# Mixtures of eight in tiles of 128 rows, second-layer weights held in SBUF, the first opening on four batches

## The reference, cut to what matters

```python
scores = xf @ Wr + br                                # 4096 tokens, 8 experts
_, top_idx = jax.lax.top_k(scores, 2)
router_weights = softmax(where(mask(top_idx), scores, -inf))
h = gelu(einsum('td,edp->etp', xf, W1) + b1[:, None, :])     # 128 -> 512, tanh form
y = einsum('etp,epd->etd', h, W2) + b2[:, None, :]           # 512 -> 128
out = einsum('te,etd->td', router_weights, y)                # x + 0.5 * out
```

## Time and profile before

| | |
|---|---|
| time, three runs | 1420.34, 1422.12, 1422.55 us; median 1422.12 |
| profiled execution | span 1422.4 us; the page gives no time around it |
| busy, share of the span | PE 83%, PEld 55%, DVE 58%, ACT 51%, POOL 51% |
| chain that ended last | PE 54%, DVE 14%, POOL 10%, DMA 8%, issue 6%, ACT 5%, SP's queue 3% |
| first mixture of eight on TensorE | about 77 to 242 us |
| second mixture of eight on TensorE | about 718 to 893 us |

### The profile page before, as it was taken

The page is one execution under the profiler, slowest core; times in us unless marked ns, Lnnn a source line. Parts: engine busy times, 40 slices in busy tenths (PEclk is TensorE's granted clock), DMA queues, the critical chain, the costliest instruction groups (busy, mean ns, idle before and its releaser), DMA issues.

```text
span 1422.4 us, 23037 instructions
## 1 busy us (share of the span) xinstructions
PE 1176.4 (83%) x7234; PEld 782.2 (55%) x7234; DVE 825.7 (58%) x2697; ACT 721.3 (51%) x1451; POOL 721.7 (51%) x949
## 2 busy tenths in 40 slices
PE   4289997899999999999789998329999777389994
PEld 3278986122233232232278987218799556268894
DVE  7611265898898999998442666702216687421235
ACT  4244443477767767677544555213445575234441
POOL 3776754202424435523764477744554277625543
PEclk9999999699999999999979999659999898589997
DMA  9577887535435343341357886425577031145586
GB/s 292 149 198 213 243 234 243 163 102 167 133 103 174 103 118 118 88 136 49 117 140 222 258 234 185 146 78 167 161 211 245 28 132 36 49 133 177 175 260 199
DMA packets 166377, 226.82 MB, mean 159 GB/s; under 512 B 22960, under 2 KB 125744, under 8 KB 166256
## 3 DMA queue, kind: packets, MB, share of 16 engines
q1 hardware_dynamic: 121456, 174.04, 42.3%
q0 software_dynamic: 18304, 37.65, 7.7%
q10 hardware_dynamic: 26496, 13.64, 3.3%
HBM read 152.81 MB, written 72.20 MB: 158 GB/s over the span
## 4 chain that ended last, share of the span: by engine, by line
PE 54%; DVE 14%; POOL 10%; DMA 8%; issue 6%; ACT 5%; SPq 3%; ACTq 0%; POOLq 0%; DVEq 0%
PE PS L1416 17%; PE PS L1406 16%; POOL dispatched L736 8%; DVE arena L2300 5%; PE PS L1584 5%; PE PS L1560 5%; DMA arena<-experts 3%; ACT arena L1131 2%; PE PS L1396 2%; PE PS L1568 2%; PE PS L1546 2%; DMA YC<-expert_out 1%; DVE BST L1858 1%; DVE X L1868 1%; DMA expert_out<-arena 1%
## 5 line engine op out<-in xcount | busy, mean ns | idle before, releaser
L1004 ACT ACTIVATE arena<-PS,arena 128x256 f32<-128x256 f32 (+1 forms) x568 | 267.4, 498 | 367.7 <-PE PS L1406 355.8
L764 POOL DMA_INDIRECT expert_out<-arena x316 | 304.5, 964 | 281.7 <-issue 192.9
L1131 ACT ACTIVATE arena<-PS 128x512 f32<-128x512 f32 x512 | 283.9, 596 | 134.8 <-PE PS L1560 133.9
L2300 DVE TENSOR_REDUCE arena<-PS 128x2 f32<-128x1024 f32 x256 | 300.9, 1217 | 28.8 <-PE PS L1570 27.9
L1406 PE MATMUL PS<-arena 128*128 128x256 f32 (+1 forms) x1136 | 309.0, 415 | 9.8 <-DMA arena<-experts 7.5
L1416 PEld LDWEIGHTS PS<-arena 128*128 128x128 f32 x2528 | 303.9, 192 | 18.7 <-issue 4.0
L1416 PE MATMUL PS<-arena 128*128 128x128 f32 x2528 | 306.7, 275 | 3.2 <-DVE arena L2123 3.2
L2123 DVE TENSOR_TENSOR arena<-PS,arena 128x256 f32<-128x256 f32 (+1 forms) x142 | 64.5, 454 | 369.5 <-PE PS L1416 369.5
L1406 PEld LDWEIGHTS PS<-arena 128*128 128x128 f32 x1136 | 210.0, 195 | 59.8 <-DMA arena<-experts 10.1
L736 POOL DMA_INDIRECT dispatched<-arena x192 | 185.3, 965 | 81.7 <-issue 57.9
L1560 PE MATMUL PS<-arena 96*128 96x512 bf16 x512 | 174.2, 391 | 10.5 <-ACT arena L1131 4.7
(11 more groups left out here) (274 smaller groups left out, 1177.3 us busy)
## 6 DMA issues: line engine op xcount, KB each, us to landing
arena<-experts SPq DMA_DIRECT2D x142, 578.0 KB
qk_products<-arena SPq DMA_DIRECT2D x48, 384.0 KB, 4.4
arena<-qk_products SPq DMA_DIRECT2D x64, 288.0 KB
arena<-dispatched SPq DMA_DIRECT2D x110, 129.0 KB, 3.0
dispatched<-FILL SPq DMA_DIRECT2D x32, 322.5 KB, 2.8
YC<-expert_out ACTq DMA_DIRECT2D x40, 256.0 KB
arena<-qk_products SPq DMA_DIRECT2D x64, 128.0 KB, 5.1
arena<-dispatched SPq DMA_DIRECT2D x32, 193.5 KB, 4.0
```

Of the source, the lines that this page charges most:

```text
L764: pool.indirect_dma_start(YK, bass.IndirectOffsetOnAxis(ap=ID[:, s:s + 1], axis=0), YS[:, s, :], None).then_inc(s_yo[r], 16)
L1004: act.activation(HT[:, tau % PAIR, q, 0:S * P], hidden_chunk(S, q), func, bias=WE[:, r, 2 * DFF + q:2 * DFF + q + 1]).then_inc(s_g, 1)
L1131: act.activation(PT[:, G % 2, j, k, :], bank(4 + k % 2), ACT.Exp, scale=float(1.0 / np.sqrt(HD))).then_inc(s_exp, 1)
L2300: dve.tensor_reduce(MX[:, G % 2, head:4:2, a], PS[:, 1024 * w:1024 * w + 1024].rearrange("p (a b) -> p a b", a=2), AX_X, ALU.max).then_inc ...
```

## The change

Tiles of the mixtures of eight have 128 rows (`S0 = 1`), so there are 71. Each expert's second-layer weights (262 KB) are loaded once for each mixture to a fixed place in SBUF: for the first mixture at the start, before anything is cleared, for the second in the last groups of the attention. The table holds the place of these weights instead of the expert's number; TensorE loads it into a register for each tile and addresses the moving operand of the second layer by it. SP takes the expert from the row number (regions now have 8192 rows) and issues three DMAs for a tile: rows, biases (behind the rows in the same ring) and first-layer weights. Weights are asked for when the hidden layer of the tile four before is done. The 16 clears move from the opening into the loop of the first mixture, the stores of the first attention batch behind the loop, the loads of expert outputs in mid-mixture from ACT to SP, the filling of the stacks from POOL to DVE. The first mixture opens on four batches and 25 tiles, the second on 12 tiles; all steps laid between tiles are spread over twice the number, POOL sends one block for a tile. At the end of the attention the table of all tiles is computed in three parts between tiles. Two tiles share a scatter semaphore.

The diff, cut to its core:

```diff
-E0, S0 = 8, 2
+E0, S0 = 8, 1
...
-REGION = TOKENS + S0 * P
+REGION = 2 * TOKENS
...
-KNOWN = 5
-SOON = 12
+KNOWN = 4
+SOON = 25
 LEAD = 4
-BEGUN = 6
+BEGUN = 12
...
+SPLIT_AT, RING_AT, BEHIND_AT = 35062, 12310, 26754
+PLACES = [[RING_AT + RING * UP + DOWN * n for n in range(5)] + [BEHIND_AT + DOWN * n for n in range(3)],
+          [SPLIT_AT + DOWN * n for n in range(E0)]]
...
             if b >= NG - 2:
-                return MOE[0]["tiles"] + 1 + 2 * (b - NG + 2)
+                return MOE[0]["tiles"] + 1 + 4 * (b - NG + 2)
             if carries(L):
-                return max(tiles_to(b) + 4, early_tiles(L) + E0 + 3 + 2 * b)
-            return max(tiles_to(b) + 6, early_tiles(L) + E0 + 4 + 2 * b)
+                return max(tiles_to(b) + 8 + b, early_tiles(L) + E0 + 6 + 4 * b)
+            return max(tiles_to(b) + 12, early_tiles(L) + E0 + 10 + 4 * b)
...
         @block.sync
+            def expert_stays(f, e):
+                at = PLACES[first_kind(f)][e]
+                sp.dma_start(arena[:, at:at + DOWN], ex0_in[e, :, UP:UP + DOWN]).then_inc(s_stay, 16)
+
+            for e in range(E0):
+                expert_stays(0, e)
             sp.wait_ge(s_zero, 1)
             sp.wait_ge(s_fill0, 1)
-            for e in range(E1):
-                clear_experts(BUFS[1], e, s_cleared)
...
+            def eight(L):
+                def rows_in(tau):
+                    if tau < tiles:
+                        r = tau % XRING
+                        t, n = (TS0, tau) if tau < soon else (TS, tau - soon)
+                        row = sp.value_load(t[n:n + 1, 0:1], min_val=0, max_val=E0 * REGION - S0 * P)
+                        found[tau] = row // REGION
+                        sp.dma_start(XP[:, r, 0, :], BUFS[0][bass.ds(row, P), :]).then_inc(s_rows[r], 16)
+                        sp.dma_start(biases(f, tau), ex0_in[bass.ds(found[tau], 1), :, UP + DOWN:WROW]
+                                     .rearrange("o p n -> p (o n)")).then_inc(s_rows[r], 16)
+
+                def ups_in(tau):
+                    sp.dma_start(ups(f, tau), ex0_in[bass.ds(found[tau], 1), :, 0:UP].rearrange("o p n -> p (o n)"))                      .then_inc(s_we[tau % RING], 16)
+
+                def follow(tau, rows=True):
+                    sp.wait_ge(s_h, (T0 + tau - (RING - 1)) * FC)
+                    ups_in(tau)
+                    if rows:
+                        sp.wait_ge(s_yc, T0 + tau - RING)
+                        rows_in(tau + XRING - RING - 1)
...
+                lead = XRING - RING - 1
+                for tau in range(RING):
+                    rows_in(tau)
+                    ups_in(tau)
+                for tau in range(RING, RING + lead):
+                    rows_in(tau)
+                clear_tails()
+                for tau in range(RING, soon - lead):
+                    follow(tau)
...
+                for tau in range(soon - lead, tiles):
+                    follow(tau)
+                    if f == 0 and 0 <= tau - soon < E1:
+                        clear_experts(BUFS[1], tau - soon, s_cleared)
+                    for b in range(combined_within(L)):
+                        if start_of(L, b) == tau:
+                            wait_outputs(sp, f, outputs_of(L, b))
+                            load_outputs(sp, L, b)
+                if prepares(L):
+                    first_stacks()
+                    sp.wait_ge(s_fill, 2 * QK_RING)
+                    sp.wait_ge(s_qd, STORES)
+                    load_stacks(0)
+                for b in (NG - 2, NG - 1):
+                    wait_outputs(sp, f, outputs_of(L, b))
+                    load_outputs(sp, L, b)
...
         @block.gpsimd
-                    for n in range(2 if tau < tiles - 4 else 0):
-                        if carries(L) and place_of(L, sent // (2 * GT)) <= tau:
-                            send_next(sent)
-                            sent += 1
+                    if carries(L) and tau < tiles - 8 and place_of(L, sent // (2 * GT)) <= tau:
+                        send_next(sent)
+                        sent += 1
...
         @block.tensor
+            def find_expert(f, tau, soon):
+                stays[f, tau] = pe.value_load(stay_of(tau, soon), min_val=0, max_val=ARENA - DOWN)
+
+            def downs(f, tau, q):
+                if moe_of(f)["E"] == E0:
+                    return arena[:, bass.ds(stays[f, tau] + q * D, D)]
+                return WE[:, tau % RING, UP + q * D:UP + q * D + D]
...
                         mm = pe.matmul(bank(6, P * s, P * s + P), HT[:, tau % PAIR, q, P * s:P * s + P],
-                                       WE[:, r, DFF + q * D:DFF + q * D + D], start=(q == 0), stop=(q == FC - 1))
+                                       downs(f, tau, q), start=(q == 0), stop=(q == FC - 1))
...
                     if c <= tiles:
                         outputs(c - 1)
+                        find(c + 1)
...
         @block.vector
-                rows_turned(f, 1)
-                main_table(f, bank(5, 0, NG * E0), True)
+                main_counts(f, bank(5, 0, NG * E0), True)
                 rows_turned(f, 2)
                 outputs_out(f, 0)
+                main_sums()
+                rows_turned(f, 3)
+                outputs_out(f, 1)
+                main_rows(f)
+                rows_turned(f, 4)
+                outputs_out(f, 2)
                 even_gates(f)
```

More of the change, by code:

```diff
@@ L110, in constants @@
     put("spare", PAIRS + np.arange(BLOCKS)[None, :] * P + p[:, None])
-    put("segrow", np.append(np.tile(np.arange(E0) * REGION, NG), E0 * REGION))
-    put("segstep", np.tile(np.where(np.arange(E0) < E0 - 1, 1, 1 - E0), NG) * (np.arange(NG * E0) < NG * E0 - 1))
+    put("segrow", np.append(np.tile(np.arange(E0) * REGION, NG), SPARE_AT))
+    for n, places in enumerate(PLACES):
+        steps = np.tile(np.roll(places, -1) - np.array(places), NG)
+        put(f"segplace{n}", steps * (np.arange(NG * E0) < NG * E0 - 1))
     put("tile", p[:, None])
@@ L239, in build @@
         behind = cv.at
+        assert behind == BEHIND_AT
         cv = Carver()
@@ L373, in row_loads, with each, stay_of, biases @@
         def row_loads(f, tau):
-            before = sum(len(range(tau % XRING, moe_of(j)["tiles"], XRING)) for j in range(f))
-            return (tau % XRING < XCHUNKS) + before + tau // XRING + 1
+            def each(j):
+                return 2 if moe_of(j)["E"] == E0 else 1
+            before = sum(each(j) * len(range(tau % XRING, moe_of(j)["tiles"], XRING)) for j in range(f))
+            return (tau % XRING < XCHUNKS) + before + each(f) * (tau // XRING + 1)
+        def stay_of(tau, soon):
+            t, n = (ET0, tau) if tau < soon else (ET, tau - soon)
+            return t[n:n + 1, 0:1]
+        def biases(f, tau):
+            if moe_of(f)["E"] == E1:
+                return WE[:, tau % RING, UP + DOWN:WROW]
+            return XP[:, tau % XRING, 1:3, :].rearrange("p a b -> p (a b)")[:, 0:NARROW]
+        def ups(f, tau):
+            if moe_of(f)["E"] == E1:
+                return WE[:, tau % RING, 0:UP]
+            return arena[:, RING_AT + UP * (tau % RING):RING_AT + UP * (tau % RING + 1)]
         def scattered0(f, r):
@@ L381, in scattered, with shared_by, sign_of @@
         def scattered(f, r, n):
-            return sum(16 * size(f, tau) for tau in range(r, n, out_ring(f)))
+            return sum(16 * size(f, tau) for tau in range(n) if sign_of(f, tau) == r)
+        def shared_by(f):
+            return PAIR if moe_of(f)["E"] == E0 else 1
+        def sign_of(f, tau):
+            return tau % out_ring(f) // shared_by(f)
         def out_ring(f):
@@ L636, in moe @@
[L636 to L645, removed]
@@ L659, in moe @@
-                if f == 0:
-                    sp.wait_ge(s_cleared, CLEARED)
-                for tau in range(soon, XRING if not soon else ahead + XRING - RING):
+                for tau in range(RING):
+                    expert_in(tau)
+                sp.wait_ge(s_disp, sent_for(L))
+                for tau in range(XRING):
                     rows_in(tau)
-                for tau in range(max(ahead, RING), tiles):
+                for tau in range(RING, tiles):
                     sp.wait_ge(s_yc, T0 + tau - (RING - 1))
@@ L711, in attention @@
                         store(b + 1)
+                    if 0 <= G - (GROUPS - 6) < 4:
+                        sp.wait_ge(s_qd, STORES * NG)
+                        for e in range(2 * (G - (GROUPS - 6)), 2 * (G - (GROUPS - 6)) + 2):
+                            expert_stays(ffn_of(L + 1), e)
             for L, kind in enumerate(SUBLAYERS):
-                if kind in (FFN0, FFN1):
-                    moe(L)
+                if kind == FFN0:
+                    eight(L)
+                elif kind == FFN1:
+                    sixteen(L)
                 elif kind == ATTN:
@@ L1499, in open_keys_values, with find @@
                     mm.then_inc(s_lk, 1)
+                def find(tau):
```

(5 more changed lines are left out.)

267 lines of the change are left out of this document (127 added, 140 removed).

## The result

The changed kernel takes 1466.78 us (median of four runs, 1463.23 to 1469.38), the kernel before 1421.59 beside it: ratio 1.0295, interval 1.026 to 1.033. The forecast had the sign and the engine, but 18 us where 45 came.

What follows compares the result with a forecast made beforehand. TensorE bounds the mixtures at 3.73 us per tile; after the change SP was to pace them at 2.32. First mixture +14.6 us and second +3.2 sum to 17.8, so 1440 us, range 1402 to 1468.

Steps and rivals of the forecast that it cites:

- SP paces: Both mixtures: SP's register load and three issues take 2.32 us per tile, over TensorE's 1.89; chance above break-even 0.67.
- no waits of SP in either mixture: Sign that the forecast is right: SP issues without waiting in both mixtures, three issues each 2.3 us.
- the first rival: Both mixtures: issues overlap or cost under 1.89 us per tile, so TensorE sets the pace; 1399 us, chance 0.18.
- Break-even at 2.2: Rival for SP's pace in both mixtures: at 2.2 us per tile nothing is won or lost, 1422 us; chance 0.08.
- 6 loads of outputs: First mixture, SP's queue: six loads of expert outputs formerly issued by ScalarE, estimated at 1.3 us each, 7.8 in all.
- the 16 clears moved from the opening into the loop: First mixture, SP's queue: each clear costs an issue and a gap of 0.44 us, 7 us in all.
- All these fit into 2.32 us per tile: Items put at nothing, among them ScalarE's and VectorE's work per tile, stay hidden; at 1.89 they would begin to show.
- The stores: End of first mixture: six stores of the first attention batch behind the loop, 3.4 us of issues and a landing of 6.
- The second mixture: Last weights leave SP at 893.7, last bias add 900.2, then POOL's 38 sends until 948.3: +3.2 us.
- The opening: First mixture opens on four batches, 32 sends instead of 40, so SP's wait ends at 60.8 instead of 70.92.
- TensorE paces: Faster rival, both mixtures: issues cost under 1.89 us per tile, each mixture 11.4 us shorter; 1399 us, chance 0.18.
- Exposed register loads: Rival, both mixtures: TensorE's register load and addresses add 1.14 us per tile, 3.03 in all; 1541 us, chance 0.07.

Runs made afterwards that it cites:

- the extra issue: The changed kernel with one more 16-byte DMA issue of SP per tile, into a place nothing reads: 1533.53 us.
- the unchecked loads: The changed kernel with SP's and TensorE's register loads without their range check, every DMA kept: 1443.99 us.
- The two experiments at its end: Second mixture's last three batches added two steps later, on the changed kernel: 1468.91 us; POOL sending behind its last eight scatters too, on the SP-relieved kernel: 1427.22 us.
- the same edit: The kernel before, with the first mixture opened on four batches and nine tiles of 256 rows (second on four batches too): 1423.8 us, ratio 0.9998.
- with SP relieved: The changed kernel with biases and first-layer weights in one DMA, clears at the opening, output loads on ScalarE, SP's tails later: 1424.39 us, ratio 1.0003.

## Why the prediction was right in kind and wrong in size

POOL's last send came 25 us later than forecast: 13.6 of them lie before the second group of maxima, 2.1 under the rest of the attention, where nothing was forecast, and 9.3 in the second mixture. What cost the 2.1 is open.

**SP paces.** Right: step 2.20 against 2.32 forecast, no wait in quiet tiles, TensorE's gaps in the first mixture mostly ended by weights. Of the signs named, "no waits of SP in either mixture" did not hold: it waited for bias adds ten times in the first. The rule of the Trainium skill (DMA: Bandwidth & Descriptors, "Issuing engines are not separate DMA queues"), that the issue is usually small relative to the DMA, holds for one transfer here too (0.33 us of issue, 3.33 to landing). For a stream of them it would have forecast the first rival, and the extra issue and the unchecked loads show what it leaves out: a tile's 2.2 us on SP is under one landing and above TensorE's 1.89.

**Break-even at 2.2.** Wrong, and plainly so: 2.20 came, and the kernel lost 45 us. The point had been worked out with the other terms of SP's queue as forecast. They failed. It was luck that the step came out shorter than forecast: its 8.5 us over 71 tiles hid as much of what the other terms cost. From SP's start at 60.50 to the last weights, as read from the trace:

| term of the first mixture | forecast | trace |
|---|---|---|
| 71 tiles | 164.7 | 156.2 (71 x 2.20) |
| 4 tails | 4.6 | 4.4 |
| 16 clears | 7.0 | 15.8: issues and gaps 9.3, longer register loads 6.5 |
| longer register loads in other tiles | 0 | 1.1 |
| 6 loads of outputs | 7.8 | 7.7 |
| waits for bias adds | 0 | 5.2 |
| issues over their 0.33 us | 0 | 5.4 (213 issues) |
| sum | 184.1 | 195.8 (60.50 to 256.3) |

**The failed step** is "the 16 clears moved from the opening into the loop, an issue and a gap of 0.44 each, 7". An issue of a clear takes 0.43 to 2.11 us, and the next register load, mostly 0.27 us elsewhere, takes 0.46 to 0.94 (one of sixteen 0.28). So the clears cost 15.8 us where 7 were forecast, and taking them out gave 12.6 back. The price was that of one rows issue with its gap; no row read there shows a clear between the loads of a mixture.

**"All these fit into 2.32 us per tile"** failed second. VectorE's share was compared as an average; but its work on a batch comes in blocks, and the tile period had shrunk from 3.73 to 2.2 us. In the first mixture SP waited 5.2 us for bias adds. In the second, VectorE is busy without a gap from 929.74 to 940.0, its bias adds up to 3.1 us apart, and the last one ended 13.0 us after the last weights had left (927.0 to 940.0), 6.5 forecast.

**The stores** behind the loop: stack load 12.1 us after the last weights, 9.2 forecast. Their issues alone took 6.5 us, 3.4 forecast. Together that cost 3 us.

**The second mixture** was read by the wrong chain. Its beginning was right: against the attention's end the first tail came 3.4 us later, 3.65 forecast (731 for 727.35). Its end was summed from SP's last weights through the last bias add to 38 sends. The two experiments at its end moved bias adds and sends, and it came no earlier. The row to read is POOL's, nearly full from its first send: 4.1 us of the 12.5 are that send's delay beyond the 30.3 brought in, 8.4 the two scatters more (2.5) and the idle time (5.9).

**The opening** was right: 60.50 for 60.8. That it is worth ten us is not shown: in the kernel before the same edit gave nothing, as SP then waited 8.4 us for the rest of the rows. In the changed kernel that wait does not appear, but none of its variants opens on five batches.

**The rivals.** TensorE paces, 1399: with SP relieved the time came to 1424, not 1399. By its trace a tile with its register load is 2.0 us, the waits for VectorE's copies are 13.1 us in the first mixture alone, and POOL ends the second; how the 25 us divide among these no run shows. Exposed register loads, 1541: not with one, which cost 0.1 us per tile once SP was relieved; two show the edge.

## What to carry to other kernels

When a tile is halved, divide each engine's queue by the new period before anything else: issues and register instructions per tile do not shrink with the tile. Price what is added to the queue that will be the pace at what it costs beside full DMA traffic, and give work that comes in blocks its block length against the new period, not its share. Where several engines end a stage, look for the one that is full from an earlier point on; as long as it stays full, its first instruction sets the end, not the last one of its neighbour.

## What the runs showed of the hardware that was not expected

A register load of SP is not of one length: 0.27 us in quiet tiles, 0.46 to 0.94 in fifteen of the sixteen tiles with a clear, two issues behind it. With the clears at the opening none of the 71 takes over 0.55. Checking the range of a loaded register costs SP 0.3 us per tile, and leaving the check out of SP's and TensorE's loads was worth 23 us here. TensorE's sequencer has room beside seventeen passes of 128 columns for about one register load with four addresses (2.0 us a tile instead of 1.89); two loads make the tile 2.34 us. What makes single issues take up to 2.11 us stays open, as does how much the lower granted clock in some stretches added (0.91 at 130 to 150, 1.00 there with the clears at the opening); no run here parts these.
